# Gathering the first sequence's expert rows in ascending expert order while the last experts still run

## The reference

```python
logits = x @ gate_w.T                              # layer 0, mixture of experts: 64 experts, FFN 96
scores, idx = jax.lax.top_k(softmax(logits), 8)    # 8 experts for each token
xbuf = zeros(E, C, D).at[e_sorted, pos].set(x[tok_sorted], mode='drop')
y = einsum('ecf,edf->ecd', silu(g) * u, w_down)    # g, u: two projections of xbuf
out = zeros(N, D).at[tok_sorted].add(y[e_sorted, safe_pos] * (s_sorted * valid))
x = x + out
x = x + linear_attention(layernorm(x))             # layer 1: 16 heads of 128, blocks of 32
x = x + silu(x @ w_gate.T) * (x @ w_up.T) @ w_down # layer 1 FFN (on a LayerNorm), hidden 1024
```

## Time and profile before

| | us |
|---|---|
| median of 3 runs (1488.75 to 1492.0) | 1491.08 |
| the profiled execution's own time | 1493.45 |
| its span, first to last instruction | 1491.7 |
| PE busy | 1285.2 (86%) |
| DVE busy | 1002.6 (67%) |
| ACT busy | 799.3 (54%) |
| POOL busy | 454.3 (30%) |

### The profile page before, as it was taken

How to read it: one execution, slowest core, us unless ns; L and a number is a source line. 1 busy time by engine, 2 the same in 40 slices (tenths; PEclk the granted TensorE clock), 3 DMA queues, 4 the chain that set the end, 5 groups by cost and what they waited for, 6 DMA issues and landing times.

```text
span 1491.7 us, 28462 instructions
## 1 busy us (share of the span) xinstructions
PE 1285.2 (86%) x9120; PEld 1141.4 (77%) x9120; DVE 1002.6 (67%) x2076; ACT 799.3 (54%) x1543; POOL 454.3 (30%) x495
## 2 busy tenths in 40 slices
PE   5665666059999999946999999999999999999996
PEld 4453544048888888835989989999899999998996
DVE  5665667437777777763867767667677676676665
ACT  4211221236666666633657666666666666666663
POOL 1145565721111111132632425216233251251010
PEclk9886888569999999977999999999999999999998
DMA  8992122248999999851101001001000010010000
GB/s 269 418 360 89 67 75 91 90 160 288 309 294 306 297 295 298 291 171 36 44 8 33 26 15 47 5 21 42 14 28 21 14 49 0 25 39 0 8 1 8
DMA packets 58381, 173.65 MB, mean 116 GB/s; under 512 B 10064, under 2 KB 26960, under 8 KB 56144
## 3 DMA queue, kind: packets, MB, share of 16 engines
q1 hardware_dynamic: 36096, 105.44, 20.0%
q0 software_dynamic: 21504, 67.13, 14.5%
q10 hardware_dynamic: 720, 0.28, 0.1%
HBM read 86.83 MB, written 85.98 MB: 116 GB/s over the span
## 4 chain that ended last, share of the span: by engine, by line
PE 61%; DVE 11%; DMA 11%; issue 7%; ACT 4%; POOL 3%; SPq 2%; another core or an unknown queue 1%; DVEq 0%; ACTq 0%; POOLq 0%
PE bank L788 17%; DMA experts<-in_moe_in 9%; PE bank L793 8%; PE bank L838 6%; PE bank L777 6%; PE bank L823 4%; PE bank L813 4%; PE bank L879 3%; PE bank L824 2%; PE bank L814 2%; POOL y_rows L421 2%; PE bank L708 2%; DVE experts L1470 1%; DVE experts L1483 1%
## 5 line engine op out<-in xcount | busy, mean ns | idle before, releaser
L788 PE MATMUL bank<-layer_r 128*128 128x256 f32 x2048 | 309.5, 289 | 11.1 <-issue 5.1
L1274 DVE TENSOR_TENSOR layer_r<-W,layer_r 128x1024 fp32r<-128x1024 f32 (+2 forms) x229 | 256.4, 1121 | 57.6 <-ACT layer_r L1111 57.6
L788 PEld LDWEIGHTS bank<-layer_r 128*128 128x128 f32 x2048 | 267.6, 192 | 16.0 <-issue 13.0
L1111 ACT ACTIVATE layer_r<-W 128x1024 fp32r<-128x1024 f32 (+2 forms) x226 | 221.8, 982 | 57.2 <-PE bank L838 36.7
L525 POOL TENSOR_TENSOR layer<-layer 128x256 f32<-128x256 f32 x120 | 87.4, 728 | 420.8 <-ACT layer L1186 420.4
L708 PE MATMUL bank<-experts_r 128*96 128x512 f32 x768 | 194.7, 402 | 4.4 <-DVE experts_r L1458 4.4
L498 POOL DMA_INDIRECT layer<-y_rows,layer x128 | 170.9, 1335 | 38.6 <-issue 30.4
L793 PE MATMUL bank<-layer_r 128*128 128x256 f32 x1024 | 175.7, 284 | 0.0
L708 PEld LDWEIGHTS bank<-experts_r 128*96 128x96 f32 x768 | 121.3, 163 | 53.3 <-issue 7.0
L421 POOL DMA_INDIRECT y_rows<-W x128 | 128.4, 1003 | 88.2 <-issue 55.3
L793 PEld LDWEIGHTS bank<-layer_r 128*128 128x128 f32 x1024 | 146.0, 192 | 0.0
(11 more groups left out here) (134 smaller groups left out, 2256.3 us busy)
## 6 DMA issues: line engine op xcount, KB each, us to landing
y_rows<-D SPq DMA_DIRECT2D x32, 1024.0 KB, 29.9
experts<-y_rows POOLq DMA_DIRECT2D x64, 512.0 KB, 4.4
y_rows<-experts SPq DMA_DIRECT2D x64, 512.0 KB, 4.4
W<-in_w SPq DMA_DIRECT2D x32, 416.0 KB, 5.0
experts<-in_moe_in SPq DMA_DIRECT2D x64, 192.0 KB, 4.8
experts<-in_moe_down SPq DMA_DIRECT2D x64, 96.0 KB, 4.5
y_rows<-W POOLq DMA_INDIRECT x128, 2.4
layer<-y_rows,layer POOLq DMA_INDIRECT x128, 3.0
```

What stands on the lines that cost most here:

```text
L788: pe.matmul(out, Whi1[s][:, c * step + at:c * step + at + P], x_[:, c, :], start=(n == 0 and c == 0 and x_ is hi), stop=False, skip_group_ ...
L1111: nc.scalar.activation(Whi1[i % 2][:, 0:W.shape[1]], W, ACT.Copy).then_inc(S["d_whi"], 1)
L1274: return nc.vector.tensor_tensor(dst, src, hi.bitcast(F32), ALU.subtract)
```

## The change

- `rows`, `sidx` and `wcur` get SBUF of their own, so they can be written while the experts run. To make room, the tile `PJ` of layer 0's attention moves to the region of layer 1's raw weights, which is free then.
- The columns are taken in reverse (`column`), so that k = 0 is a token's lowest expert and k = 7 its highest, for all sequences. The k-th lowest of 8 different experts out of 64 has at most the number 56 + k.
- POOL, behind `load_rows` of expert 63, copies the slots and, before column k, waits only for the stores of experts 0 to 56 + k.
- DVE adds columns 0 to 3 at the end of its steps for experts 59 to 62, column 4 between the results of 62 and 63, columns 5 and 6 behind the result of 63, all ahead of its wait for all stores; column 7 follows the split of the first two weights. The last two pairs are taken out of its loop for that, and `d_weights(0)` stands ahead of them.
- The multiplication of the output weights moves behind `d_low3(0)`; ACT waits for it ahead of `dturn(0)`, PE ahead of the output projection of head 14 of sequence 0.

```diff
-LAYER0_WORDS = 2 * (DC * HQ * 2 * SEQ + HQ * DC * 2 * P)
-LAYER1_WORDS = 10350
+LAYER0_WORDS = 2 * DC * HQ * 2 * SEQ
+LAYER1_WORDS = 10350 - 2048 - 32
+COMBINE_FROM = E - TOPK + 3
+        rows = sb("rows", [P, TB * RING, D])
+        sidx = sb("sidx", [P, TB * TOPK], I32)
+        wcur = sb("wcur", [P, TB * TOPK])
-        PJ = [take_s([HQ, DC, 2, P]) for _ in range(2)]
+        PJ = [take([HQ, DC, 2, P]) for _ in range(2)]
+        def column(t, k):
+            return t * TOPK + TOPK - 1 - k
...
 # POOL
-            for s in range(2):
-                pool.wait_ge(b_stored[s], 16 * E // 2)
-            pool.wait_ge(S["b_ya"], E)
...
-                    gather_row(t * TOPK + k, row_at(t, k))
+                    gather_row(column(t, k), row_at(t, k))
...
             slots_of(0)
             for k in range(TOPK):
+                top_expert = E - TOPK + k
+                pool.wait_ge(b_stored[0], 16 * (top_expert // 2 + 1))
+                pool.wait_ge(b_stored[1], 16 * ((top_expert + 1) // 2))
                 gather_rows(0, k)
...
 # PE
-            pe.wait_ge(S["w1o_scaled"], 1)
             pe.wait_ge(S["l1_loaded"], 16 * W1_PIECES)
...
                     terms = [(gD, None)]
+                    if isinstance(b, int) and b == 0 and h == OUT_SPLIT:
+                        pe.wait_ge(S["w1o_scaled"], 1)
...
 # ACT
-            act.wait_ge(S["w1o_scaled"], 1)
             d_high3(0)
             d_front(0, False, range(1))
+            act.wait_ge(S["w1o_scaled"], 1)
             dturn(0, True, False)
...
 # DVE
                     b_result(e - 1, 1 - s)
                     b_down(e + 1, 1 - s)
+                    if isinstance(e, int) and e >= COMBINE_FROM:
+                        d_combine(0, e - COMBINE_FROM)
...
             b_pair(0)
-            with dve.Fori(1, E // B2 - 1) as i:
+            with dve.Fori(1, E // B2 - 3) as i:
                 b_pair(i)
+            d_weights(0)
+            b_pair(E // B2 - 3)
+            b_pair(E // B2 - 2)
             b_mul(E - 1, 1)
             b_rest(E - 1, 1)
             b_result(E - 2, 0)
+            d_combine(0, E - 1 - COMBINE_FROM)
             b_result(E - 1, 1)
+            for k in range(E - COMBINE_FROM, TOPK - 1):
+                d_combine(0, k)
             for s in range(2):
                 dve.wait_ge(b_stored[s], 16 * E // 2)
             dve.wait_ge(S["b_ya"], E)
...
-            dve.wait_ge(S["norm_loaded"], 16)
-            for h in range(H1):
-                ins = nc.vector.tensor_scalar(out_weights(h), ...)
-            ins.then_inc(S["w1o_scaled"], 1)
...
-            d_weights(0)
-            for k in range(TOPK):
-                d_combine(0, k)
+            d_combine(0, TOPK - 1)
             d_norm3(0)
             d_low3(0)
+            dve.wait_ge(S["norm_loaded"], 16)
+            for h in range(H1):
+                ins = nc.vector.tensor_scalar(out_weights(h), ...)
+            ins.then_inc(S["w1o_scaled"], 1)
             dturn(0, True, True, False)
```

More of the change, by code:

```diff
@@ L239, in build @@
         take, take_r = stage(("layer1", LAYER1_WORDS, F32), ("layer1_r", LAYER1_R_WORDS, F32R))
-        rows = take([TB * RING, D])
-        sidx = take([TB * TOPK], I32)
         xh3 = take([TB, D])
@@ L247, in build @@
         vD = take([TB, C1])
-        wcur = take([TB * TOPK])
         PD = [take([3, P]) for _ in range(2)]
@@ L476, in _ @@
                     load_rows(i * B2 + s, s)
-            for s in range(2):
-                pool.wait_ge(b_stored[s], 16 * E // 2)
-            pool.wait_ge(S["b_ya"], E)
             def slots_of(b):
-                pool.tensor_copy(sidx, SLOT[:, b, :] if isinstance(b, int) else
+                pool.tensor_copy(sidx[:], SLOT[:, b, :] if isinstance(b, int) else
                                  SLOT[:, bass.ds(b, 1), :].rearrange("p a n -> p (a n)")
@@ L1484, in b_result, with d_combine, d_weights @@
                                       ).then_inc(S["b_yb"], 1)
+            def d_combine(b, k):
+                for t in range(TB):
+                    dve.wait_ge(d_row[column(t, k)], b * 16 + 16)
+                if k:
+                    dve.wait_ge(S["d_comb_steps"], b * COMB_STEPS + TB * k)
+                for t in range(TB):
+                    c = column(t, k)
+                    nc.vector.scalar_tensor_tensor(
+                        out=xtile(b, t), in0=rows[:, row_at(t, k), :], scalar=wcur[:, c:c + 1],
+                        in1=xtile(b, t), op0=ALU.mult, op1=ALU.add).then_inc(S["d_comb_steps"], 1)
+            def d_weights(b):
+                after(dve, "d_comb_steps", b * COMB_STEPS)
+                nc.vector.tensor_scalar(wcur[:], WGT[:, b, :] if isinstance(b, int) else
+                                        WGT[:, bass.ds(b, 1), :].rearrange("p a n -> p (a n)"),
+                                        1.0, None, ALU.mult).then_inc(S["d_wcur"], 1)
+                dve.wait_ge(S["d_wcur"], b + 1)
             def b_pair(i):
@@ L1543, in _ @@
                 split_weights(0, V_USE + i)
-            dve.wait_ge(S["norm_loaded"], 16)
-            for h in range(H1):
-                ins = nc.vector.tensor_scalar(out_weights(h), out_weights(h), nrm[:, h:h + 1], 0.5,
-                                              ALU.mult, ALU.mult)
-            ins.then_inc(S["w1o_scaled"], 1)
[L1550 to L1568, removed]
             def d_norm3(b):
@@ L1659, in dturn @@
                         d_gate(b, h)
-            d_weights(0)
-            for k in range(TOPK):
-                d_combine(0, k)
+            d_combine(0, TOPK - 1)
             d_norm3(0)
             d_low3(0)
+            dve.wait_ge(S["norm_loaded"], 16)
+            for h in range(H1):
+                ins = nc.vector.tensor_scalar(out_weights(h), out_weights(h), nrm[:, h:h + 1], 0.5,
+                                              ALU.mult, ALU.mult)
+            ins.then_inc(S["w1o_scaled"], 1)
             dturn(0, True, True, False)
```

## The result

The changed kernel takes 1482.63 us, the median of 5 runs (1480.03 to 1484.22), against 1491.22 us for 5 runs of the kernel before: a ratio of 0.994, with a 95% interval of 0.9923 to 0.9956. It is 8.6 us faster, where 10 were forecast; the predicted time was 1481. Its profiled execution took 1484.22 us.

The account below looks back on a forecast made before the run. POOL's issue of 16 gathers was taken to bound the seam. Removing fourteen gave 20.5 us, less what early additions cost the experts: gain 10, 1483.4 us from the profiled execution, 1481 from the median; range 1474 to 1489.

Parts of the forecast that it names:

- The first wait: DVE's step for expert 59: waits for column 0's gather, landing 3.7 us; DVE 6.6 us late, PE idle about 5.
- Additions 1 to 3: DVE's next three expert steps: 5.59 us each with an addition, 16.8 against 15.6; product of expert 63 7.8 us late.
- The clock: PE's gap in the experts: clock probably falls, next 4 to 6 us at 1.2 GHz; mostly hidden, 0.4 us put.
- The tail: From expert 63's product: column 4 fits DVE's wait, stores move 8.2 us, column 7 starts at 669.6, 10.2 us earlier.
- The scaling: Output weights' multiplication (4.49 us) behind the low part in layer 1: just fits, costs nothing; uncovered, at most 4.49 us.
- The rest: Tiles' new places, two unrolled pairs, slots' reversal: one more small DVE instruction; nothing, bounds 0.4 us either way.
- A: Rival: the stall at column 0 is absorbed and stores stay in place; gain 18 us, time 1473; chance 0.10.
- B: Rival: DMA engines are the bound, early gathers delay weights and stores by 5.9 us; gain 4, 1487; chance 0.12.
- C: Rival: PE's clock stays at 1.2 GHz to the end of the experts; gain 2.5 us, 1488.5; chance 0.08.
- D: Rival: slower, additions wait for gathers in the experts; landings from 7.4 us lose, at 8.5 us 1494.5; chance 0.06.

Follow-up runs that it names:

- E6: Changed kernel with a quarter of POOL's row load of expert 63, 128 KB in place of 512, ahead of the first gathers: 1482.39 us, one execution.
- E7: Changed kernel with the 416 KB piece of layer 1's weights issued beside the first gathers loaded at the start of the experts instead: 1485.29 us, one execution.
- E8: E1 with DVE's two splits ahead of columns 6 and 7 and the last two layer 1 weight pieces loaded at the experts' start: 1473.86 us.
- E1: Changed kernel with every addition two expert steps later, column 0 at the end of DVE's step for expert 61: 1475.7 us.
- E5: Changed kernel with the scaling of the output weights back at the seam, ahead of the last addition and behind the two splits: 1487.77 us.
- E3: Changed kernel with gathers and additions back behind all stores, tile places, reversed columns, unrolled pairs and moved scaling kept: 1489.97 us.
- E4: Changed kernel with no addition inside the expert steps; gathers of columns 0 to 3 still early, column 0 added between the last two results: 1476.97 us.

## Why the prediction was right, step by step

The forecast of a gain of 10 us, 20.5 at the seam less 10 in the experts, was right in mechanism and sign, and by the medians 1.4 us too large. The two profiles had reached the last experts at different times, so the steps are counted from the transposes of expert 61 (629.05 before, 625.97 after).

| step | forecast, us from there | measured |
|---|---|---|
| column 0 added | 8.6 | 11.6 |
| product of expert 63 | 26.8 | 28.7 |
| store of 62 issued | 29.6 | 31.5 |
| first gather of column 6 | 33.0 | 36.3 |
| column 7 added | 40.6 | 43.5 |

- **The first wait** was named at its place, with PE's gap behind it; its size was the term that failed. The landing was put at 3.7 us, within 2.8 to 4.4, and took 6.3; the wait was 7.9 us and not 5.6, PE's gap 8.3 and not 5. The range came from gathers at the seam, at a mean DMA share of 0.29, and in layer 1, at 0.06 to 0.09 (windows from 700 us on). The share of 0.91 that spoke of the place moved the figure only from the seam's median to its maximum. E6 and E7 point to it as the price. In the trace of before POOL's ten row loads of 512 KB between 580 and 660 us showed that landings there are longer and spread more:

```profile
DMA to landing us min/median/max: 3.7/4.4/6.6
```

- **Additions 1 to 3**: steps of 5.43 us against 5.59. Right; this gave 0.5 us back.
- **The clock** fell in the gap and was back some 3 to 4 us after PE resumed. The transposes took 1.97 and the hidden layer 3.91 us, 1.04 and 3.0 in the step before, and DVE's steps stayed at 5.4: hidden whole, where 0.4 was put.
- **The tail**: column 4 did not fit. Its addition began 2.27 us behind DVE's copy, and the copy of the last result after it. The trace has the landing of one gather of that pair only, 3.2 us; the other, issued at 654.21, took at most the 5.45 us to DVE's start. The store of 62 was 4.8 us from its issue to column 6's first gather (3.4 forecast): 3.9 to its landing, and 0.9 from there to the gather's start. Late gather and late store lie beside a weight piece of layer 1 that SP issues at 654.09. E8, which loads that piece early, has 3.6 us for the second gather of the pair and 2.6 for the store; E1, which does not, has 5.2 and 3.3. The longer way from store to gather cost 1.4 us, and the splits ahead of column 7 stood last, as forecast.

```profile
654.09 0.42 SPq L395 DMA_DIRECT2D W<-in_w  x1
...
654.21 1.02 POOL L497 DMA_INDIRECT rows<-y_rows,sidx  x1 [0.30 <-issue]
...
657.47 4.09 SPq L378 DMA_DIRECT2D y_rows<-experts  x2
...
659.66 0.88 DVE L1497 SCALAR_TENSOR_TENSOR X<-rows,wcur,X 128x256 f32<-128x256 f32 x2 [2.27 <-issue]
...
662.26 1.00 POOL L497 DMA_INDIRECT rows<-y_rows,sidx  x1 [1.89 <-DMA y_rows<-experts]
```

- **The scaling** needed its new place (E5) and cost nothing there.
- **The rest.** In this sum the seam gained 7.3 us: 54.9 from the transposes of 61 to those of layer 1 before, 47.6 after. The profiles differ by 9.2 because the execution after was 3.1 us earlier at the start of that stretch, and 1.2 longer in layer 1. Neither is shown to be the change's. The length of layer 1 goes with the moment at which the clock rises (last section). The start varies: E3, without the early gathers, began its experts at 308.72 us as the changed kernel did (308.98), E4, with them, at 311.09, the kernel before at 311.24; and E5, which is the changed kernel up to the seam, took 315.0 us from there to the transposes of 61, the changed kernel 317.0, the kernel before 317.8. So the forecast was 2.7 us too large for the stretch that it summed, and that the medians miss it by 1.4 only is in part luck: the interval of the runs, a gain of 6.6 to 11.5 us, holds both 7.3 and 10.
- **Rivals.** A (18 us) is refuted for the kernel as it is: the stall was not absorbed. E1, which has no stall, shows what A stood for: 15.5 us. B had the cause that E6 and E7 point to and the wrong place: in the changed kernel ACT waits 0.19 us for weights at 629.96 and no longer after that, while DVE waits 7.90 for a gather. C is refuted, the clock was back at 644. D did not come to pass, but its chain was there: at 6.3 us in all places it would have left 3 us; after the first pair the columns landed in 2.7 to 5.6 us, and one of its signs stood there, the 2.27 us for which column 4 held DVE.

## What to carry to other kernels

A transfer moved into a busy stretch is priced by a transfer in that stretch, never by the same instruction in an idle one. Work that waits for it goes far enough behind its issue: where early issue takes most of the wait away, the consumer need not move with it (E4), and a consumer put too early in an in-order engine gives back what the early issue gained (E1). When the longest thing of a stretch is taken away, the work that it hid (the scaling, E5) has to be moved too.

## What the runs showed of the hardware that was not expected

- The same 128-row gather landed in 2.8 us at the quiet end of the seam and in 6.3 to 7.1 us with the DMA share at 0.95 (5.8 to 6.3 at the same place in E1, E4 and E5), while POOL's issue of the first six stayed at 1.0 to 1.1 us.
- The start of layer 1 differs by up to a microsecond from one execution to the next, by when the clock rises after the seam. The second silu of ACT, which waits for PE, came 4.64 us after the first value matmul before, 4.99 in E4, 5.29 after, and 5.58 in E1, E3 and E5; the clock was back 3.4 us after that matmul before, 4.0 in E4, 4.6 after, and 5.4 to 6.0 in the other three; from the transposes to the end these executions took 807.8, 808.5, 808.9, and 809.0, 809.4 and 809.7 us. What sets the moment of the rise stays open.
- In E1 a gather at 633.02 took 1.00 us beside a subtraction of DVE with both inputs in SBUF (633.16, 0.69 us); in the kernel before one took 1.88 beside a longer one. The Trainium skill, "SBUF — State Buffer", section "Who interferes with whom", has it that such an instruction was not seen to stall descriptor writing. The first row agrees and the second does not. Beside an addition, which has two inputs in SBUF as well, one gather took 1.63 us in the changed kernel (648.17, the addition at 648.45) and one 1.00 in E1 (651.96, 652.10): such a neighbour alone does not decide it, and no run here tells what does.
